# AdaLN block with a gated cumulative-sum attention and a two-group expert layer: the order of independent groups in one step, on ScalarE, GpSimd and VectorE

## The reference, cut to what matters

```python
mod = (silu(c) @ wmod).reshape(8, 6, 1, 512)                 # sa, ca, ga, sb, cb, gb
h = layernorm(x) * (1 + ca) + sa                             # x: 8 x 2048 x 512, float32
xn = layernorm(h) * ln_gamma + ln_beta
k, v, r = xn @ Wk.T, xn @ Wv.T, xn @ Wr.T
kv = k * v
csum = cumsum(kv * sigmoid(time_decay) ** t, axis=time)
wkv = sigmoid(time_first) * kv + sigmoid(time_decay) * shifted(csum)
x = x + ga * ((sigmoid(r) * wkv) @ Wo.T)
h = layernorm(x) * (1 + cb) + sb
for group in (0, 1):                                         # 32 experts each, top 2 of softmax
    route(h @ router_w)                                      # sort tokens by expert
    y = (silu(xs @ wg[e]) * (xs @ wu[e])) @ wd[e]            # per expert, 512 -> 256 -> 512
    out_g = scatter_add(y * weight)
x = x + gb * (out_0 + out_1) / 2
```

## Time and profile before

| | |
|---|---|
| median of 3 runs | 4848.11 us |
| profiled execution | 4859.97 us, its span 4858.2 us |
| TensorE, VectorE busy in the span | 4561.6 us (94%), 3056.9 us (63%) |
| GpSimd, ScalarE busy in the span | 2856.0 us (59%), 1655.1 us (34%) |
| TensorE, VectorE busy from 178.5 to 1777.6 us | 1536.23 and 1524.94 of 1599.10 us |
| GpSimd, ScalarE busy in the same stretch | 1224.19 and 750.15 us |

### The profile page before, as it was taken

One profiled execution on the slowest core, in us unless ns is written; L12 is line 12 of the kernel. 1 busy time (PEld: TensorE's weight loads), 2 busy tenths in 40 slices (PEclk: granted clock), 3 DMA queues, 4 the chain that ended last, 5 costly groups with the idle time before them and its releaser, 6 DMA issues.

```text
span 4858.2 us, 89097 instructions
## 1 busy us (share of the span) xinstructions
PE 4561.6 (94%) x22649; PEld 3757.8 (77%) x22649; DVE 3056.9 (63%) x6077; ACT 1655.1 (34%) x4221; POOL 2856.0 (59%) x2303
## 2 busy tenths in 40 slices
PE   6999999999999993989999998999999999999998
PEld 4878778787878773877777777888788888888886
DVE  5999999999999994444444444544344444444443
ACT  2445444444444441322222222332222222222222
POOL 2677777777777775444545454555455555555554
PEclk8999999999999996999999999999999999999999
DMA  6767676766767676899999989998998988998887
GB/s 242 237 202 241 200 227 207 219 218 210 230 200 223 203 231 206 231 285 255 260 284 269 286 243 285 273 291 201 296 243 233 248 232 229 266 239 222 210 216 193
DMA packets 434618, 1152.40 MB, mean 237 GB/s; under 512 B 59362, under 2 KB 59363, under 8 KB 415667
## 3 DMA queue, kind: packets, MB, share of 16 engines
q0 software_dynamic: 182512, 454.27, 40.3%
q1 hardware_dynamic: 231106, 619.79, 37.7%
q10 hardware_dynamic: 20736, 75.51, 4.2%
HBM read 719.35 MB, written 463.57 MB: 243 GB/s over the span
## 4 chain that ended last, share of the span: by engine, by line
PE 45%; DMA 11%; issue 3%; POOL 1%; DVE 1%; POOLq 0%; SPq 0%; DVEq 0%; ACT 0%
PE ps L1321 13%; PE ps L1323 13%; PE ps L1322 13%; DMA out<-c_yo,c_idx 10%; PE ps L1330 4%; PE ps L1349 2%; DMA c_wt<-wsp_d 1%; POOL out L1312 1%; POOL c_xg L1279 0%; DVE c_yo L1576 0%; POOL list_d L1284 0%; POOLq L1304 0%; DMA list_d<-pairs,sidx 0%; DMA c_lists<-list_d,c_rowu 0%; DVE c_xl L1564 0%
## 5 line engine op out<-in xcount | busy, mean ns | idle before, releaser
L1312 POOL DMA_INDIRECT out<-c_yo,c_idx x576 | 914.8, 1588 | 928.3 <-DMA out<-c_yo,c_idx 475.9
L1321 PE MATMUL ps<-c_wt,c_xh 128*128 128x512 f32 x2304 | 965.6, 419 | 22.6 <-issue 15.1
L1323 PE MATMUL ps<-c_wt,c_xl 128*128 128x512 f32 x2304 | 910.7, 395 | 0.0
L1322 PE MATMUL ps<-c_wt,c_xh 128*128 128x512 f32 x2304 | 904.8, 393 | 0.0
L1279 POOL DMA_INDIRECT c_xg<-h2g_d,c_idx x576 | 566.4, 983 | 519.8 <-DVE c_yo L1576 413.5
L1560 DVE TENSOR_TENSOR c_hh<-ps,c_sil 128x256 f32<-128x256 f32 x576 | 244.4, 424 | 913.7 <-ACT c_sil L1403 849.0
L1576 DVE SCALAR_TENSOR_TENSOR c_yo<-ps,c_wc,c_xg 128x512 f32<-128x512 f32 x576 | 432.5, 751 | 538.7 <-DMA out<-c_yo,c_idx 266.5
L1408 ACT CAST c_xh<-ps 128x512 fp32r<-128x512 f32 x576 | 339.3, 589 | 972.9 <-PE ps L1330 911.7
L711 POOL DMA_INDIRECT list_d<-pairs,sidx x496 | 547.6, 1104 | 186.1 <-issue 124.8
L444 PE MATMUL ps<-xTh,wTh 128*128 128x512 f32 x1536 | 621.5, 405 | 34.5 <-DVE xTl L820 16.8
L1403 ACT ACTIVATE c_sil<-ps 128x256 f32<-128x256 f32 x576 | 221.5, 384 | 1175.2 <-PE ps L1323 1125.0
(11 more groups left out here) (203 smaller groups left out, 7753.4 us busy)
## 6 DMA issues: line engine op xcount, KB each, us to landing
c_wt<-wsp_d SPq DMA_DIRECT2D x69, 2048.0 KB
sraw<-wex SPq DMA_DIRECT2D x290, 256.0 KB
wsp_d<-shigh SPq DMA_DIRECT2D x288, 256.0 KB
wsp_d<-sraw SPq DMA_DIRECT2D x288, 256.0 KB
c_wt<-wsp_d SPq DMA_DIRECT2D x69, 1024.0 KB
xin<-x SPq DMA_DIRECT2D x34, 1024.0 KB
h2g_d<-mod_d SPq DMA_DIRECT2D x128, 256.0 KB
out<-xin SPq DMA_DIRECT2D x32, 1024.0 KB
```

The lines of the kernel that those rows point to most:

```text
L1312: nc.gpsimd.indirect_dma_start(out=out, out_offset=bass.IndirectOffsetOnAxis(ap=idx[:, n:n + 1], axis=0), in_=yo[:, n % 4, :], in_offset=N ...
L1321: nc.tensor.matmul(o, lh, rh, start=first, stop=False)
L1322: nc.tensor.matmul(o, lh, rl, start=False, stop=False)
L1323: return nc.tensor.matmul(o, ll, rh, start=False, stop=last)
```

## The change

The three `step` functions of stage A call the same groups in another order; no group is changed, added or removed, and the code before and after the loop is the same.

```diff
--- before.py
+++ after.py
@@ -618,37 +618,37 @@
             def step(b, s, first):
                 back_too = not (first and s == 0)
                 at = s * PER_STEP
+                if not (first and s < 2):
+                    soften(b, s - 2)
                 chunk_k(b, s, 0)
                 stage_hi(b, at)
                 stage_hi(b, at + 1)
                 chunk_r(b, s, 0)
-                if not (first and s < 2):
-                    soften(b, s - 2)
+                stage_hi(b, at + 2)
+                chunk_k(b, s, 1)
+                stage_hi(b, at + 3)
                 hi(b, s, 0)
-                stage_hi(b, at + 2)
-                stage_hi(b, at + 3)
+                chunk_r(b, s, 1)
+                stage_hi(b, at + 4)
+                stage_hi(b, at + 5)
                 normed(b, s)
-                stage_hi(b, at + 4)
-                chunk_k(b, s, 1)
-                stage_hi(b, at + 5)
-                chunk_r(b, s, 1)
                 chunk_k(b, s, 2)
+                stage_hi(b, at + 6)
+                hi(b, s, 1)
+                chunk_k(b, s, 3)
                 if back_too:
                     turned(b, s)
-                hi(b, s, 1)
-                stage_hi(b, at + 6)
+                stage_hi(b, at + 7)
                 chunk_r(b, s, 2)
-                chunk_k(b, s, 3)
+                front(b, s, (0, 1))
+                stage_hi(b, at + 8)
+                chunk_r(b, s, 3)
                 hi(b, s, 2)
-                stage_hi(b, at + 7)
-                stage_hi(b, at + 8)
-                stage_hi(b, at + 9)
-                front(b, s, (0, 1))
-                chunk_r(b, s, 3)
                 front(b, s, (2, 3))
-                hi(b, s, 3)
                 if back_too:
                     logits(b, s)
+                stage_hi(b, at + 9)
+                hi(b, s, 3)
 
             normed(0, -1)
             front(0, -1, range(KC))
@@ -715,36 +715,36 @@
             def step(b, s, first):
                 old = not (first and s < 2)
                 at = s * PER_STEP
+                stage_lo(b, at)
                 rstd(f_var, vaf, h_ready, rsf, f_rstd, b, s + 1)
                 if not (first and s < 3):
-                    scatter(b, s - 3, 11, 16)
-                stage_lo(b, at)
+                    scatter(b, s - 3, 11, 15)
+                stage_lo(b, at + 1)
                 receive(b, s, 0)
-                stage_lo(b, at + 1)
-                lo(b, s, 0)
+                if not (first and s < 3):
+                    scatter(b, s - 3, 15, 16)
+                stage_lo(b, at + 2)
                 rstd(g_var, vag, z_ready, rsg, g_rstd, b, s + 1)
-                stage_lo(b, at + 2)
                 stage_lo(b, at + 3)
                 if not (first and s == 0):
                     rstd(b_var, vab, h2_ready, rsb, b_rstd, b, s - 1)
                 if old:
-                    scatter(b, s - 2, 0, 7)
+                    scatter(b, s - 2, 0, 4)
+                lo(b, s, 0)
                 receive(b, s, 1)
                 if old:
-                    scatter(b, s - 2, 7, 8)
+                    scatter(b, s - 2, 4, 7)
                 lo(b, s, 1)
+                stage_lo(b, at + 7)
                 receive(b, s, 2)
                 if old:
-                    scatter(b, s - 2, 8, 9)
+                    scatter(b, s - 2, 7, 8)
+                stage_lo(b, at + 8)
+                receive(b, s, 3)
                 lo(b, s, 2)
-                stage_lo(b, at + 7)
-                stage_lo(b, at + 8)
+                stage_lo(b, at + 9)
                 if old:
-                    scatter(b, s - 2, 9, 10)
-                stage_lo(b, at + 9)
-                receive(b, s, 3)
-                if old:
-                    scatter(b, s - 2, 10, 11)
+                    scatter(b, s - 2, 8, 11)
                 lo(b, s, 3)
 
             rstd(f_var, vaf, h_ready, rsf, f_rstd, 0, 0)
@@ -941,22 +941,22 @@
                 V.tensor_copy(sidx[:, u, :].rearrange("p (r k) -> p k r", k=2), slf[:]).then_inc(slot_ready, 1)
 
             def step(b, s, first):
-                norm_front(b, s + 1, 1)
                 if not (first and s < 2):
                     topk(b, s - 2)
+                norm_front(b, s + 1, 1)
                 chunk(b, s, 0)
                 norm_front(b, s + 1, 2)
                 if not (first and s == 0):
                     residual(b, s - 1)
-                norm_front(b, s + 1, 3)
                 if not (first and s < 2):
                     place(b, s - 2)
+                norm_front(b, s + 1, 3)
                 if not (first and s == 0):
                     modulate(b, s - 1)
+                chunk(b, s, 1)
                 stage_lo(b, s * PER_STEP + 4)
-                chunk(b, s, 1)
+                chunk(b, s, 2)
                 stage_lo(b, s * PER_STEP + 5)
-                chunk(b, s, 2)
                 stage_lo(b, s * PER_STEP + 6)
                 norm_front(b, s + 2, 0)
                 chunk(b, s, 3)
```

## The result

The changed kernel takes 4785.62 us (median of 4 runs, 4780.55 to 4789.95) against 4852.72 of the kernel before on the same chip (4839.39 to 4858.83). The ratio is 0.9861, with a 95% interval of 0.9847 to 0.9876. That is 67 us less; 60 were forecast. The profiled execution is the one of 4789.95 us, 70.0 less than the profiled one of before.

What follows compares the result with a forecast made beforehand. TensorE and VectorE, both near full, wait for each other in stage A: 106.8 us of waits, less 32.4 at the back edge, leaves 74.4. Less 14 for GpSimd's last product gives 60: 4848.11 to 4788 us, range 4766 to 4830.

Steps and rivals of the forecast that it cites:

- (4): GpSimd's last L701, done S+7.5, wanted S+8.5 (S: TensorE's first projection): 0 to 1.1 us wait per step, priced 14 us.
- the 74 us: Stage A's TensorE waits that a new order could win back: 106.8 us less 32.4 at the back edge.
- The 32 us of the back edge: TensorE's loop back edge, passed six times: some 5.4 us each, gap plus slow matmuls, which no order gives back.
- (1): VectorE ahead of chunk 1's scan: less stretching and a moved subtraction save 2.2 to 3.5 us per step.
- (2): VectorE's end of step: L885 less stretched, gain 1.5 us less 0.6; input split at S+48.5 to S+49.8, before S+52.6.
- (3): ScalarE's end of step: job 8's cast at S+48 after its load, L616 not held, margin over 1 us.
- Start and tail: First two steps gain 0 to 4 us, the tail loses about 1; both left out of the sum.
- nothing moves: Rival: TensorE's and ScalarE's hand-overs cause the waits before L466, so VectorE would only wait; 4840 to 4855, chance 0.08.
- half of it: Rival: GpSimd's products meet other VectorE operations and each step keeps a wait; gain 20 to 45 us, chance 0.15.
- The slower one: Rival: GpSimd's last product comes late, TensorE waits 2.7 us at about 4.5 per step; 4904, chance 0.09.

Runs made afterwards that it cites:

- e7: The changed kernel with five scatters instead of three directly ahead of GpSimd's last product L701, as many in all: 4848.51 us, ratio 1.0003 to the kernel before.
- e1: The kernel before with VectorE's order new, ScalarE's and GpSimd's old: 4877.96 us, ratio 1.0064.
- e2: The kernel before with ScalarE's and GpSimd's orders new, VectorE's old: 4882.16 us, ratio 1.0069.
- e5: The kernel before with VectorE's order new and, on ScalarE, weight job 9's cast moved behind L616: 4874.42 us, ratio 1.0059.
- e6: The kernel before with ScalarE's and GpSimd's orders new and, on VectorE, only `topk` moved ahead of `norm_front` part 1: 4795.31 us, ratio 0.9897.
- e10: The kernel before with only VectorE's subtractions of jobs 4 and 5 moved behind chunks 1 and 2: 4885.67 us, ratio 1.0072.
- e11: The kernel before with VectorE's order new and ScalarE's end of the step new, GpSimd's order old: 4858.92 us, ratio 1.0017.
- e4: The kernel before, old order, with GpSimd's products (except those of the output weights) on 8 of 512 columns: 4804.13 us, ratio 0.9906.
- e3: The changed kernel with three of the four scatters beside L797 moved later, so that GpSimd's products run beside L797 again: 4797.30 us, ratio 0.9897.
- e9: The kernel before with only `topk` moved ahead of `norm_front` part 1 on VectorE: 4841.56 us, ratio 0.9986.

## Why the prediction was right

The frame held to a few tenths: 29 steps of 51.46 us and what the back edge adds. The remainder was put at 32 + 14 = 46 us and is 1528.6 - 1492.3 = 36.3. Two terms of it were mis-sized, in opposite directions. They left the stage's gain 10 us above the forecast, 70.5 against 60. That 4788 and 4785.62 lie so close is in part luck: the profiled execution came out 10 us under the 4800 forecast for it, and the 11.9 us between profile and median, carried over from before, turned out 4.3.

- **The 14 us of (4)** are 0. The last L701 ended at S+7.9 for the forecast S+7.5, one third scatter taking 1.34 beside L791, and the matmul on `woh` started at S+8.30 unhindered. The margin was overstated (0.8, really 0.4) and the extra delay too. Charging the middle of an interval from 0 to 1.1 us for a threshold that was not crossed is what made the sum 14 too low. The Trainium skill (SBUF — State Buffer, "Who interferes with whom") infers that VectorE's `tensor_tensor` doesn't hold up the generating of a DMA's descriptors. The prediction drew a wait of 0 from that, which doesn't follow: the inference speaks of the scatters only, while the last product L701 reads SBUF and could still meet L791, as it did. And the trace doesn't bear the inference out for these scatters, which read their indices from SBUF: one took 1.34 instead of 0.97, and the margin swallowed it. So the 74 us are nearer to the 70.5 than my 60, but not by that rule. e7 shows that with the product 2.5 us later nearly every step pays.
- **The 32 us of the back edge** are 36. At 915.04 the gap is 3.01, and with the 2.0 us for slow matmuls of the earlier trace rows that makes 5.0; but the two steps about it are 5.6 us over the clean ones. The other 0.6 is there when starts are compared with starts: the step before 915.04 takes 54.67 us, 3.2 over, since the view counts the gap only from the end of the last matmul, and the step behind it 53.85, 2.4 over, since besides the ten slow matmuls the first one is 0.59 us ahead of the second, where 0.32 is usual (968.89), and the one behind the ten is slow in part. Most of the six are like that or a little longer.
- **(1)** came out earlier than its range: scan at S+34.1 for S+34.6 to 35.9, and not for the reasons given alone. L797 is as forecast (747) and gave 2.1 us of the 2.4. L791 was to fall below 900 and stayed at 1001, since the last L701 reaches it, so its 1.0 didn't come. L871 runs undisturbed (741 ns), so the 1.3 charged there wasn't due, but it was 756 before, so nothing was gained there either. What made up for L791 is a term that the sum doesn't have: VectorE begins the step 1.3 us earlier, since (2) shortens the end of the step before.
- **(2)** job 4's subtraction at S+34.8, the split of the next input at S+47.6, both 1 us earlier than forecast; L885 at 742 instead of 900: of 58 only two are stretched (1.8 and 3.0 us).
- **(3)** the cast of job 8 at S+47.9 (forecast S+48), no wait for its load; ScalarE's waits for these loads fell from 110.6 us to 0.3. The hand-over went to ScalarE as said: VectorE waits 1.39 for the second pair.
- Start and tail, forecast at +4 to -1, are next to nothing: 70.0 us of the execution against 70.5 of the stage.

Rivals: "nothing moves" and "half of it" are out by the steps. The slower one has its mechanism shown by e7, with a price of 2.2 us per step for 2.1 of wait. The prediction's 4.5 was for 2.7 of wait and had slow matmuls behind every one; its sentence that the clock falls from gaps of over 2 us holds for only 12 of e7's 21 such gaps before `woh`, and not for all of before either: behind gaps of 2.29 us at 544.30 and 1209.31 the transposes run at full pace.

What the prediction didn't see is how the parts hang together, and so three of my expectations on parts of the change (e1, e2, e5) had the wrong sign. It summed them as gains of VectorE. In fact VectorE's order alone costs 27 us, the two others' alone 31, and together they gain 67 (24, 18 and 70.5 in the 29 steps). The coupling is in two places: `soften` first on ScalarE needs `topk` first on VectorE (e2, e6), and later subtractions need ScalarE's weight casts behind L616 (e1, e10, e11). e4 shows that with the products cut short the old order is as fast in stage A as the new one, though not how much of that is contention and how much is GpSimd's shorter row. That the contention isn't all is shown by e3, where L797 is stretched again for 12 to 17 us, and by e2, where most of it is gone without a gain.

## What to carry to other kernels

Where engines hand work around in a fixed order, price a change of the orders by the starts of the bottleneck's steps against its cleanest step, and never price one engine's part by itself: for each group moved later, follow its buffer to the load and the cast, and ask what stands behind that cast. A stretch beside another engine's work costs only what is beyond the slack, so a threshold term is either 0 or the full excess: compute the margin and state both outcomes with their chances, rather than one value between them. When every ordinary step is at the bottleneck's own time, look at the loop itself: written out, it gave another 25 to 35 us here.

## What the runs showed of the hardware

- The stretching depends on the moment, not on the operation: with `topk` moved ahead of it and nothing else changed (e9), L791 fell from 993 to 746 ns. Mostly it comes whole or not at all: from 400 to 1640 us the shortest L797 of before takes 0.74 us and the median one 1.78, and a mean of 1347 ns mixes the two; in the changed kernel none takes over 0.79.
- It can span two instructions of the other engine: the L885 of 2.97 us at 1046.47 ended only after both products beside it.
- A GpSimd scatter took 0.96 to 0.99 us in most rows, and 1.34 beside L791 (1025.59), 1.49 beside L871; but 0.97 at 1024.32 with L791 beside its second half.
- Behind 21 gaps of TensorE of 2.04 to 2.41 us in one trace (e7) the matmuls ran 0.43 us apart in 12 cases and 0.23 in nine, and gaps of equal length (2.40 at 789.87 and 1013.36) went both ways.
- A back edge of the loop costs TensorE 3.0 to 3.5 us of nothing in five of six cases, and VectorE 22.0 us in six; with the loop written out no gap of this kind is in the trace.
